# Logarithms of 2048 small matrices: Jacobi sweeps replaced by simultaneous turns of all pairs, as 32x32 products on TensorE

## The chip, the cores and the metric

The kernel runs on one core of one Trainium2 chip, in f32 except where said. The metric is device time in microseconds. Before the change the median of 3 runs is 18,431.96 us (18,423.55 to 18,440.54).

## The reference, cut to what matters

```python
x = x + _L0_conv_ref(_gn(x), gamma, beta)        # x: 16 x 128 x 32 x 32
t = _to_tokens(x)
t = t + _L1_attn_ref(_ln_t(t), Wq, Wk, Wv, Wo, bo)
t = t + _L1_ffn_ref(_ln_t(t), ...)

def _L0_conv_ref(X, gamma, beta):
    Xf = X.reshape(B * K, s, s)                  # 2048 matrices, 32 x 32
    w, V = jnp.linalg.eigh(Xf)                   # takes the symmetric part
    w = jnp.clip(w, 1e-8)
    L = jnp.einsum('nij,nj,nkj->nik', V, jnp.log(w), V)
    mean_log = jnp.mean(L, axis=0)
    Lc = gamma * (L - mean_log) + beta
    return the same with exp in place of log, of Lc
```

`_gn` is a group normalisation over 4 channels. The attention (top 32 of 1024 keys) and the layer of experts are the same in both kernels.

## The kernel before, in words

The five engines run programs of their own, which wait on semaphores; the order on each engine is the written one. `hold(eng, sem, value)` (line 56) is a wait and an increment of a counter, two instructions. Loops are hardware loops (`Fori`) on each engine. A matmul in f32 stands in the trace as two records, each with a weight load of its own; in bf16 as one.

`normalise` (line 148) loads x as 128 channels x 16 images x 1024 elements, computes the group statistics, adds the transpose, scales, and takes the column norms of every matrix twice (`column_norms`, line 111), to shift the diagonal.

`jacobi` (line 230) works on all 2048 matrices at once, one channel to a partition, in two halves of 8 images: 6 sweeps of 31 turns, each turn rotating 16 disjoint pairs of columns. DVE forms the products of paired columns (line 329), PE sums them over the rows by 32 products with the identity (line 390), POOL and ACT compute the rotation's coefficients on small tiles (lines 435 to 517), DVE applies them (lines 342 and 352) to six images of a half and PE with ACT to two (lines 401 and 428).

`logarithm` (line 530) takes the eigenvalues from the column norms, scales the columns, turns the layout (line 616: four images to the 128 partitions, 32 rows each) and forms each logarithm as a product of 32x32 (`quad_products`, line 636: 16 columns blocks x 4 blocks of rows, 64 products of 32x32 to a bank). At its end DVE sums over all matrices (line 605).

`exponential` (line 646) uses the same `quad_products` in 16 tiles of 128 matrices with 10 steps of 2 halves (64 products each): a polynomial and seven squarings. `back_to_channels` (line 764) turns the layout back. Attention and experts follow.

Of the kernel before, what the change touches and what calls it, by code (L numbers as in the profile page):

```python
# [17 lines left out]
BY_PE = 2  # L18
PAIRS = S // 2
ROUNDS = S - 1  # L20
SWEEPS = 6
# [3 lines left out]
TINY = 1e-30  # L25
TINY_LOG = 1e-18
# [51 lines left out]
def constants(nc, mem):  # L78

    with ExitStack() as ctx:  # L80
# [4 lines left out]
        def _(pool):  # L85
# [3 lines left out]
            nc.gpsimd.memset(mem.tiny[:], TINY).then_inc(filled, 1)  # L89
            nc.gpsimd.memset(mem.eps_gn[:], EPS_GN).then_inc(filled, 1)  # L90
            for tile, value in ((mem.minus_tiny, -TINY), (mem.tiny_log, TINY_LOG), (mem.one, 1.0), (mem.two, 2.0)):
                nc.gpsimd.memset(tile[:], value)
            hold(pool, filled, 5)
# [6 lines left out]
            hold(pool, filled, 7)  # L100
# [3 lines left out]
            for d in range(-3, 4):  # L104
                hold(pool, filled, 8 + d + 3)
                nc.gpsimd.affine_select(out=mem.quad_mean[:], in_=mem.quad_mean[:], compare_op=ALU.not_equal,
                                        fill=1.0 / (B * P), base=S * d, pattern=[[-1, P]],
                                        channel_multiplier=1).then_inc(filled, 1)

def column_norms(nc, mem, sems, base):

    squares_ready, squares_used, norms_summed = sems

    def act_part(act, source_ready, ready_at, norms_ready):
        for c in range(4):
            act.wait_ge(source_ready, ready_at[c // 2])
            if c >= 2:  # L120
                act.wait_ge(norms_summed, base * 4 + c - 1)
            nc.scalar.activation(mem.product[c % 2][:, :].rearrange("p (m n) -> p m n", m=4),
                                 mem.even[:, 4 * c:4 * c + 4, :], ACT.Square).then_inc(squares_ready, 1)
            if c >= 1:
                collect(act, c - 1, norms_ready)
        collect(act, 3, norms_ready)

    def collect(act, c, norms_ready):
        act.wait_ge(norms_summed, base * 4 + c + 1)
        nc.scalar.activation(mem.weights[:, c // 2, 0, 4 * (c % 2):4 * (c % 2) + 4, :],  # L130
                             mem.dots[c % 2][:, 0:4 * S].rearrange("p (m j) -> p m j", m=4),
                             ACT.Copy).then_inc(norms_ready, 1)

    def pe_part(pe, norms_ready, ready_base):
        for c in range(4):
            hold(pe, squares_ready, base * 4 + c + 1)
            if c >= 2:
                hold(pe, norms_ready, ready_base + c - 1)
            sq = mem.product[c % 2][:, :].rearrange("p (mj r) -> p mj r", r=S)
            for r in range(S):  # L140
                last = nc.tensor.matmul(mem.dots[c % 2][:, 0:4 * S], mem.ident[:], sq[:, :, r],
                                        start=(r == 0), stop=(r == S - 1))
            last.then_inc(norms_summed, 1)

    return act_part, pe_part

def normalise(nc, mem, x_dram):

    with ExitStack() as ctx:
# [5 lines left out]
        norm_sems = (sem("prep_squares"), None, sem("prep_norms"))  # L157
        norms_ready = sem("prep_norms_ready")
        sums = ctx.enter_context(nc.sbuf_tensor("sums", [P, 4, B], F32))
        ps = mem.dots[0]  # L160
# [7 lines left out]
        @block.tensor  # L168
        def _(pe):
            hold(pe, step, 1)  # L170
            nc.tensor.matmul(ps[:, 0:B], mem.group[:], sums[:, 0, :], start=True, stop=True).then_inc(pe_done, 1)
            pe.wait_ge(squared, B)
            nc.tensor.matmul(ps[:, B:2 * B], mem.group[:], sums[:, 1, :], start=True, stop=True).then_inc(pe_done, 1)
            column_norms(nc, mem, norm_sems, 0)[1](pe, norms_ready, 0)
            column_norms(nc, mem, norm_sems, 1)[1](pe, norms_ready, 4)

        @block.scalar
        def _(act):
            act.wait_ge(step, 2)
            scratch = mem.work[:].rearrange("p s (m n) -> p (s m) n", n=N)  # L180
            for m in range(B):
                if m >= 12:
                    act.wait_ge(squared, m - 11)
                nc.scalar.activation(scratch[:, m % 12, :], mem.even[:, m, :], ACT.Square,
# [3 lines left out]

            column_norms(nc, mem, norm_sems, 0)[0](act, step, (6, 6), norms_ready)
            act.wait_ge(step, 7)  # L190
            nc.scalar.activation(sums[:, 3, :], sums[:, 2, :], ACT.Sqrt, bias=mem.tiny[:]).then_inc(act_done, 1)

            column_norms(nc, mem, norm_sems, 1)[0](act, step, (9, 9), norms_ready)

        @block.vector
        def _(dve):
# [21 lines left out]
            dve.wait_ge(norms_ready, 4)  # L218
            for h in range(2):
                last = nc.vector.tensor_reduce(sums[:, 2, HB * h:HB * h + HB], mem.weights[:, h, 0], AX.X, ALU.add)  # L220
            last.then_inc(step, 1)
            dve.wait_ge(act_done, 2)
            nc.vector.tensor_scalar(mem.shift[:], sums[:, 3, :], 1.1, 1e-4, ALU.mult, ALU.add).then_inc(step, 1)
            dve.wait_ge(step, 8)
            diag = mem.even[:, :, 0:N:S + 1]
            nc.vector.tensor_tensor(diag, diag, mem.shift[:].rearrange("p (m n) -> p m n", n=1).broadcast_to([P, B, S]),
                                    ALU.add).then_inc(step, 1)

def jacobi(nc, mem):  # L230

    with ExitStack() as ctx:
# [3 lines left out]
        def small(name, *shape):  # L241
            return ctx.enter_context(nc.sbuf_tensor(name, [P, 2] + list(shape), F32))

        twice_dot = small("twice_dot", HB, PAIRS)
        weighed = small("weighed", HB, 2, PAIRS)
        cross = small("cross", HB, PAIRS)
        half_cross = small("half_cross", HB, PAIRS)
        gap = small("gap", HB, PAIRS)
        radicand = small("radicand", HB, PAIRS)
        root = small("root", HB, PAIRS)  # L250
        gap_abs = small("gap_abs", HB, PAIRS)
        gap_sign = small("gap_sign", 2, HB, PAIRS)
        inverse = small("inverse", HB, PAIRS)
        ratio = small("ratio", 2, HB, PAIRS)
        coef = small("coef", HB, 2, PAIRS)
        secant = small("secant", HB, PAIRS)
        cosine = small("cosine", HB, PAIRS)
        moved = small("moved", 2, HB, S)
        scale = small("scale", HB, S)

        prod_ready = [sem(f"prod_ready{h}") for h in range(2)]
        dots_done = [sem(f"dots_done{h}") for h in range(2)]
        dot_read = [sem(f"dot_read{h}") for h in range(2)]
        cross_ready = [sem(f"cross_ready{h}") for h in range(2)]
        gap_ready = [sem(f"gap_ready{h}") for h in range(2)]
        root_ready = [sem(f"root_ready{h}") for h in range(2)]
        sum_ready = [sem(f"sum_ready{h}") for h in range(2)]
        inverse_ready = [sem(f"inverse_ready{h}") for h in range(2)]
        act_step = sem("act_step")
        coef_ready = [sem(f"coef_ready{h}") for h in range(2)]  # L270
        sec_ready = [sem(f"sec_ready{h}") for h in range(2)]
        cos_ready = [sem(f"cos_ready{h}") for h in range(2)]
        moved_ready = [sem(f"moved_ready{h}") for h in range(2)]
        weights_ready = [sem(f"weights_ready{h}") for h in range(2)]
        part_ready = [sem(f"part_ready{h}") for h in range(2)]
        rotated_ready = [sem(f"rotated_ready{h}") for h in range(2)]
        rotated_out = [sem(f"rotated_out{h}") for h in range(2)]
        ones_ready = sem("ones_ready")
        left_over = sem("left_over")
        scale_log = sem("scale_log")  # L280
        scale_ready = sem("scale_ready")
        scaled = sem("scaled")
        norms_ready = sem("norms_ready")
        norm_sems = (sem("squares_ready"), None, sem("norms_summed"))
        dve_step, pool_step = sem("dve_step"), sem("pool_step")
        DVE_STEPS, POOL_STEPS, ACT_STEPS = 8, 18, 6

        def columns(buf, h):
            return buf[:, HB * h:HB * h + HB, :].rearrange("p m (j r) -> p m j r", r=S)

        def paired(buf, h):
            return buf[:, HB * h:HB * h + HB, :].rearrange("p m (s j r) -> p m s j r", s=2, r=S)

        def swapped(t):
            return t[:, :, ::-1]

        def over_sides(t):
            return t.rearrange("p m (s j) -> p m s j", s=1).broadcast_to([P, HB, 2, PAIRS])

        def twice(t):  # L300
            return t.rearrange("p m (s j) -> p s m j", s=1).broadcast_to([P, 2, HB, PAIRS])
# [1382 lines left out]
```

## Time and profile before

| | us |
|---|---|
| median of 3 runs | 18,431.96 |
| span of the profiled execution | 18,450.5 |
| Jacobi turns | 11,292.3 |
| exponential | 1,300.2 |
| PE busy over the span | 13,662.3 |
| DVE busy over the span | 10,991.9 |

The execution that was profiled has its span, from first to last instruction, as its only time; it stands 18.5 us over the median of the runs. Busy times of PE are modelled at their ends and overlap with its weight loads (PEld).

### The profile page before, as it was taken

What the parts mean: (1) busy time and instruction counts of PE and PEld (TensorE: products, weight loads), DVE (VectorE), ACT (ScalarE), POOL (GpSimd) and SP (SyncE); (2) the same over time, 40 slices, a digit from 0 to 9 for tenths busy, and PEclk for the clock granted to TensorE, in tenths of its full rate; (3) what the DMA queues carried; (4) which work ended last, traced back from release to release, by engine and by line L of the source; (5) the groups of instructions that cost most, each with busy time, mean ns of one, the idle gap of its engine ahead of it and who ended that gap; (6) DMA issues with size and microseconds to landing.
All of it is one profiled execution on the core that took longest, in us unless ns stands there. A gap on an engine that the chain in (4) does not pass through costs nothing. (4 is left out here: it accounts for less than half of the span.)

```text
span 18450.5 us, 246828 instructions
## 1 busy us (share of the span) xinstructions
PE 13662.3 (74%) x91050; PEld 8655.1 (47%) x91050; DVE 10991.9 (60%) x12977; ACT 4604.4 (25%) x10433; POOL 7006.3 (38%) x5640
## 2 busy tenths in 40 slices
PE   5777777777777777777777776444688888888888
PEld 5555555555555555555555555444322222222222
DVE  5777677767776777677767776111335445454454
ACT  2222222222222222222222222111233333333333
POOL 3666566656665666566656664000000000000000
PEclk9888888888888888888888888555789989999899
DMA  0000000000000000000000000000000000000000
GB/s 19 0 0 0 0 0 0 0 0 0 0 0 0 0 0 0 0 0 0 0 0 0 0 0 0 4 4 4 22 3 2 2 3 2 3 2 2 3 2 3
DMA packets 10095, 37.45 MB, mean 2 GB/s; under 512 B 1525, under 2 KB 3130, under 8 KB 9274
## 3 DMA queue, kind: packets, MB, share of 16 engines
q1 hardware_dynamic: 9274, 26.02, 0.4%
q8 instruction: 574, 9.40, 0.2%
q14 instruction: 247, 2.02, 0.0%
HBM read 17.63 MB, written 8.39 MB: 1 GB/s over the span
## 5 line engine op out<-in xcount | busy, mean ns | idle before, releaser
L390 PE MATMUL psum<-work,ident 128*128 128x128 f32 x23808 | 5351.9, 400 | 2810.3 <-DVE work L329 2810.3
L390 PEld LDWEIGHTS psum<-work,ident 128*128 128x128 f32 x23808 | 4999.1, 239 | 3314.4 <-issue 3100.0
L1326 DVE MAX8 w_best<-psum 128x8 f32<-128x128 f32 x8192 | 1696.3, 280 | 1012.2 <-PE psum L1221 1010.4
L491 POOL TENSOR_TENSOR gap<-weights 128x128 f32<-128x128 f32 x372 | 1955.6, 5257 | 866.5 <-ACT weights L465 472.8
L1276 PE MATMUL psum<-w_exp,w_v 128*32 128x512 f32 x4096 | 2125.5, 621 | 8.5 <-ACT w_exp L1305 7.0
L342 DVE TENSOR_TENSOR work<-even,coef 128x2048 f32<-128x2048 f32 (+1 forms) x384 | 1824.4, 4787 | 149.6 <-POOL coef L503 126.9
L329 DVE TENSOR_TENSOR work<-even 128x3072 f32<-128x3072 f32 (+1 forms) x384 | 883.8, 2305 | 1568.4 <-ACT even L428 1231.3
L342 DVE TENSOR_TENSOR work<-odd,coef 128x2048 f32<-128x2048 f32 x360 | 1718.1, 4811 | 0.0
L1305 ACT ACTIVATE w_exp<-psum 128x512 f32<-128x512 f32 x2048 | 1211.8, 597 | 1753.3 <-PE psum L1247 1753.3
L329 DVE TENSOR_TENSOR work<-odd 128x3072 f32<-128x3072 f32 x360 | 828.9, 2302 | 1306.0 <-ACT odd L428 1279.5
L401 PE MATMUL psum<-work,ident 128*128 128x512 f32 x2976 | 1524.7, 594 | 0.0
L352 DVE TENSOR_TENSOR odd<-even,work 128x384 f32<-128x384 f32 (+1 forms) x576 | 1446.8, 2562 | 26.5 <-DVE work L342 0.2
L352 DVE TENSOR_TENSOR even<-odd,work 128x5376 f32<-128x5376 f32 x540 | 1353.9, 2558 | 26.5
L493 POOL TENSOR_TENSOR weighed<-weights,twice_dot 128x256 f32<-128x256 f32 x372 | 353.0, 949 | 1993.6 <-ACT twice_dot L440 1993.6
L499 POOL TENSOR_TENSOR root<-root,gap_abs 128x128 f32<-128x128 f32 x372 | 889.0, 2390 | 386.7 <-ACT root L445 386.7
L517 POOL TENSOR_TENSOR moved<-weights,cosine 128x256 f32<-128x256 f32 x372 | 986.9, 2653 | 66.4 <-POOL cosine L516 66.4
L401 PEld LDWEIGHTS psum<-work,ident 128*128 128x128 f32 x2976 | 566.5, 190 | 718.5 <-issue 718.5
L401 PE MATMUL psum<-even,ident 128*128 128x512 f32 x1536 | 796.8, 600 | 76.6 <-DVE work L342 76.6
L1247 PE MATMUL psum<-w_q,w_k 99*128 99x512 bf16 x2048 | 806.1, 400 | 42.7 <-ACT w_q L1316 42.7
L1221 PE MATMUL psum<-w_k,w_q 96*128 96x512 bf16 x2048 | 631.1, 390 | 205.1 <-ACT w_q L1316 116.0
L1247 PEld LDWEIGHTS psum<-w_q,w_k 99*128 99x128 bf16 x2048 | 200.5, 98 | 1197.8 <-issue 1104.7
L641 PE MATMUL psum<-power 32*32 32x32 f32 x28672 | 450.9, 237 | 417.6 <-issue 401.0
(280 smaller groups left out, 13542.3 us busy)
## 6 DMA issues: line engine op xcount, KB each, us to landing
odd<-in_x SPq DMA_DIRECT2D x1, 8192.0 KB, 22.9
even<-in_x SPq DMA_DIRECT2D x1, 8192.0 KB, 24.0
out<-w_t SPq DMA_DIRECT2D x16, 512.0 KB, 4.5
w_hid<-in_fc SPq DMA_DIRECT2D x2, 256.0 KB
w_wo<-in_wo SPq DMA_DIRECT2D x8, 8.0 KB
w_wq<-in_wq SPq DMA_DIRECT2D x1, 64.0 KB
w_wk<-in_wk SPq DMA_DIRECT2D x1, 64.0 KB
w_wv<-in_wv SPq DMA_DIRECT2D x1, 64.0 KB
```

Of the source, the lines that this page charges most:

```text
L329: nc.vector.tensor_tensor(product[:, which], g[:, which, 0], g[:, which, 1], ALU.mult)\
L342: ins = nc.vector.tensor_tensor(part[:, which], partner[:, which], cb[:, which], ALU.mult)
L352: ins = nc.vector.tensor_tensor(to, a, b, ALU.add)
L390: last = nc.tensor.matmul(mem.dots[h][:, 0:P], mem.ident[:], pr[:, :, r], start=(r == 0), stop=(r == S - 1))
L401: last = nc.tensor.matmul(to, mem.ident[:], of[:, m, side].rearrange("p j r -> p (j r)"), start=(n == 0), stop=(n == 1))
L491: nc.gpsimd.tensor_tensor(gap[:, h], norm[:, :, 1], norm[:, :, 0], ALU.subtract).then_inc(gap_ready[h], 1)
L499: nc.gpsimd.tensor_tensor(root[:, h], root[:, h], gap_abs[:, h], ALU.add).then_inc(sum_ready[h], 1)
L517: nc.gpsimd.tensor_tensor(mv[:, 1], w, over_sides(cosine[:, h]), ALU.mult).then_inc(moved_ready[h], 1)
L1247: nc.tensor.matmul(banks[4 + m % 3][:], w.k[0:DEPTH + SHIFT_ROWS, 4 * g + j, P * kt:P * kt + P], w.q[0:DEPTH + SHIFT_ROWS, 4 * g + j, QB * ...
L1276: nc.tensor.matmul(banks[7][slot(j), :], w.v[:, kt, 4 * g + j, :], w.exp[m % 4][:], start=(kt == 0), stop=(kt == KT - 1)).then_inc(s.weigh ...
L1305: nc.scalar.activation(w.exp[m % 4][:], banks[4 + m % 3][:], ACT.Exp).then_inc(s.exp_done, 1)
L1326: last = nc.vector.max(w.best[:, i, o, :], banks[2 * (i % 2) + o // 4][:, P * (o % 4):P * (o % 4) + P])
```

## The change

The Jacobi sweeps, the column norms, the shift and the old logarithm are taken out. The new stage (`eigen`) first turns the layout, so that four matrices stand over each other in the 128 partitions, and works on tiles of 64 matrices (128x512). There are 4 groups of 8 tiles. Each tile gets 14 turns. In a turn, for all pairs of a matrix at once: gap and damping of each pair (two full products and two sets of 64 small ones, one of them in bf16), an angle matrix X by Ln and Exp, an orthogonal matrix J as a polynomial in X (Gram and turn: a full bf16 product and a set of 64 small ones each), then A J, J^T A J twice over for symmetry (a set and two sets), and U J (a set). Matrices in the last turn but one get a correction of U's orthogonality ("mended"). The stages of a turn are spread over slots: while tile t is at its gap, tile t-1 is at its angle, t-2 at its Gram, and so on to t-5; each engine's program goes through the slots in the written order. The turns run in two loops of 5 and 6 iterations with four bodies written out beside them, each body 8 slots. At the end of a group the logarithm is formed from U and the scaled U. The scaling in `normalise` writes `odd` in place of `even`. `exponential` and all behind it are unchanged. The diff, cut to its core:

```diff
-def column_norms(nc, mem, sems, base):
...
-            column_norms(nc, mem, norm_sems, 0)[1](pe, norms_ready, 0)
-            column_norms(nc, mem, norm_sems, 1)[1](pe, norms_ready, 4)
...
-            nc.vector.tensor_tensor(mem.even[:], mem.odd[:],
+            nc.vector.tensor_tensor(mem.odd[:], mem.odd[:],
...
-def jacobi(nc, mem):
...
-def logarithm(nc, mem):
...
+TILE = 16
+W = TILE * S
+TG = 8
+GROUPS_E = B * P // (4 * TILE * TG)
+FIRST_DAMP, LATER_DAMP = 0.25, 0.125
+FIRST_TURNS, LATER_TURNS = 6, 8
+TURNS = FIRST_TURNS + LATER_TURNS
...
+GAP, DAMP, GRAM, TURN, PROD, NEXT, VECT, MEND = range(8)
...
+def quads(nc, bank, left, right, start=True):
+    for k in range(TILE):
+        cols = slice(S * k, S * k + S)
+        for q in range(4):
+            rows = slice(S * q, S * q + S)
+            last = nc.tensor.matmul(bank[rows, cols], left[rows, cols], right[rows, cols], start=start, stop=True,
+                                    skip_group_check=not start)
+    return last
...
+AT_ANGLE, AT_GRAM, AT_TURN, AT_PROD, AT_NEXT = 1, 2, 3, 4, 5
+def slots(base, before, now):
+    def at(j, delay):
+        kind = now if j >= delay else before
+        return None if kind is None else (base + (j - delay), (j - delay) % TG, kind)
+    for j in range(TG):
+        yield j, lambda delay, j=j: at(j, delay)
...
+        def turns(eng, g, body):
+            base = g * PER
+            body(eng, g, base, None, PLAIN, 0)
+            with eng.Fori(1, FIRST_TURNS) as i:
+                body(eng, g, base + i * TG, PLAIN, PLAIN, 0)
+            with eng.Fori(FIRST_TURNS, MEND_AT) as i:
+                body(eng, g, base + i * TG, PLAIN, PLAIN, 1)
+            body(eng, g, base + MEND_AT * TG, PLAIN, MENDED, 1)
+            body(eng, g, base + (MEND_AT + 1) * TG, MENDED, PLAIN, 1)
+            body(eng, g, base + TURNS * TG, PLAIN, None, 1)
...
+            def turn(pe, g, base, before, now, which):
+                for j, at in slots(base, before, now):
+                    if at(AT_PROD) is not None:
+                        m, t, kind = at(AT_PROD)
+                        if kind == MENDED:
+                            hold(pe, mend_out, g * TG + t + 1)
+                        else:
+                            hold(pe, turned, m + 1)
+                        if not (before is None and j == AT_PROD):
+                            hold(pe, prod_out, m)
+                        quads(nc, banks[PROD], e.a[t], e.j[t % 4]).then_inc(prod_done, 1)
+                    if at(AT_NEXT) is not None:
+                        m, t, kind = at(AT_NEXT)
+                        if at(AT_PROD) is None:
+                            hold(pe, prod_out, m + 1)
+                            hold(pe, vect_out, m)
+                        turned_by = e.j[t % 4]
+                        for k in range(TILE):
+                            cols = slice(S * k, S * k + S)
+                            for left, right, first in ((turned_by, e.prod[t % 2], True), (e.prod[t % 2], turned_by, False)):
+                                for q in range(4):
+                                    rows = slice(S * q, S * q + S)
+                                    last = nc.tensor.matmul(banks[NEXT][rows, cols], left[rows, cols], right[rows, cols],
+                                                            start=first, stop=not first)
+                        last.then_inc(next_done, 1)
+                        quads(nc, banks[VECT], turned_by, e.u[t]).then_inc(vect_done, 1)
+                    if at(AT_TURN) is not None:
+                        m, t, kind = at(AT_TURN)
+                        hold(pe, mixed, m + 1)
+                        nc.tensor.matmul(banks[TURN], e.turn_eye[:], over_matrices(e.eye_bf[:]), start=True, stop=True)
+                        quads(nc, banks[TURN], e.zs[t % 2], e.mix[t % 2], start=False).then_inc(turn_done, 1)
+                        if kind == MENDED:
+                            hold(pe, turned, m + 1)
+                            hold(pe, mend_ready, g * TG + min(t + AT_TURN, TG))
+                            quads(nc, banks[MEND], e.mend[t % 4], e.j[t % 4]).then_inc(mend_done, 1)
+                    if at(AT_GRAM) is not None:
+                        m, t, kind = at(AT_GRAM)
+                        hold(pe, angle, m + 1)
+                        nc.tensor.matmul(banks[GRAM], e.gram_eye[:], over_matrices(e.eye_bf[:]), start=True, stop=True)
+                        quads(nc, banks[GRAM], e.x[t % 4], e.x[t % 4], start=False).then_inc(gram_done, 1)
+                    if at(0) is not None:
+                        m, t, kind = at(0)
+                        hold(pe, diag_ready, m + 1)
+                        if not (before is None and j == 0):
+                            hold(pe, damped, m)
+                        nc.tensor.matmul(banks[GAP], e.block_ones[:], e.diag[t % 2], start=True, stop=True)
+                        quads_by(nc, banks[GAP], e.diag[t % 2], e.minus_ones, start=False).then_inc(gap_done, 1)
+                        hold(pe, off_ready, m + 1)
+                        nc.tensor.matmul(banks[DAMP], e.damp[which][:], e.off[t % 2], start=True, stop=True)
+                        quads_by(nc, banks[DAMP], e.off[t % 2], e.damp_rows[which], start=False).then_inc(damp_done, 1)
+                        if kind == MENDED:
+                            hold(pe, flipped, g * TG + t + 1)
+                            if t >= AT_TURN:
+                                hold(pe, mend_out, g * TG + t - AT_TURN + 1)
+                            quads(nc, banks[MEND], e.flip[t % 2], e.flip[t % 2]).then_inc(length_done, 1)
...
+            def turn(act, g, base, before, now, which):
...
+                        act.wait_ge(damped, m + 1)
+                        nc.scalar.activation(e.damped[t % 2], e.damped[t % 2], ACT.Ln, bias=e.floor[:]).then_inc(log_taken, 1)
...
+                        act.wait_ge(next_done, m + 1)
+                        nc.scalar.activation(e.square[:, t], banks[NEXT], ACT.Square, scale=0.5)
+                        nc.scalar.activation(e.a[t], banks[NEXT], ACT.Copy, scale=0.5).then_inc(next_out, 1)
...
+                        act.wait_ge(log_taken, m + 1)
+                        nc.scalar.activation(e.damped[t % 2], e.damped[t % 2], ACT.Exp, scale=-1.0).then_inc(inverse, 1)
...
+                        act.wait_ge(prod_done, m + 1)
+                        nc.scalar.activation(e.prod[t % 2], banks[PROD], ACT.Copy).then_inc(prod_out, 1)
...
+                        act.wait_ge(gram_done, m + 1)
+                        nc.scalar.activation(e.zs[t % 2], banks[GRAM], ACT.Copy, scale=THIRD).then_inc(gram_out, 1)
...
+                        act.wait_ge(gap_done, m + 1)
+                        nc.scalar.activation(e.gap_sq[t % 2], banks[GAP], ACT.Square).then_inc(gap_squared, 1)
...
+            def turn(dve, g, base, before, now, which):
...
+                        dve.wait_ge(vect_done, m + 1)
+                        nc.vector.tensor_copy(e.u[t], banks[VECT]).then_inc(vect_out, 1)
...
+                        dve.wait_ge(turn_done, m + 1)
+                        nc.vector.scalar_tensor_tensor(e.j[t % 4], e.x[t % 4], ANGLE_PART, banks[TURN], ALU.mult, ALU.add)\
+                            .then_inc(turned, 1)
...
+                        dve.wait_ge(gram_out, m + 1)
+                        nc.vector.scalar_tensor_tensor(e.mix[t % 2], banks[GRAM], FOURTH / THIRD, e.x[t % 4], ALU.mult,
+                                                       ALU.add).then_inc(mixed, 1)
...
+                        dve.wait_ge(inverse, m + 1)
+                        dve.wait_ge(weighed, m + 1)
+                        nc.vector.tensor_tensor(e.x[t % 4], e.weighed[t % 2], e.damped[t % 2], ALU.mult).then_inc(angle, 1)
...
+                        dve.wait_ge(gap_squared, m + 1)
+                        nc.vector.tensor_tensor(e.weighed[t % 2], e.a[t], banks[GAP], ALU.mult).then_inc(weighed, 1)
+                        dve.wait_ge(damp_done, m + 1)
+                        nc.vector.tensor_tensor(e.damped[t % 2], e.gap_sq[t % 2], banks[DAMP], ALU.add).then_inc(damped, 1)
...
+                    nc.gpsimd.tensor_tensor(as_matrices(e.diag[t % 2]), as_matrices(e.a[t]), over_matrices(e.eye[:]), ALU.mult)\
+                        .then_inc(diag_ready, 1)
+                    nc.gpsimd.tensor_tensor(as_matrices(e.off[t % 2]), as_matrices(e.square[:, t]), over_matrices(e.not_eye[:]),
+                                            ALU.mult).then_inc(off_ready, 1)
```

Left out are the constants, the way into and out of a group, and DVE's part of the mending.

## Rows read from the trace of the kernel before

**Rows 1.** The page's header.

```profile
span 18450.5 us, 246828 instructions
```

**Rows 2.** Windows: start:end, length, busy time (instructions) by engine, clock, DMA.

```profile
236.70:11529.00 11292.30, 8264.15 (x31307) 6465.32 (x31308) 8188.77 (x2671) 2444.23 (x6777) 6982.09 (x5582) 0.85 0.00 0
11529.00:11736.50 207.50, 94.48 (x4345) 89.72 (x4345) 61.39 (x26) 28.46 (x48) 1.89 (x10) 0.60 0.01 3
11736.50:13036.70 1300.20, 644.92 (x40960) 597.42 (x40960) 135.00 (x127) 172.06 (x288) 0.00 (x0) 0.50 0.02 4
```

**Rows 3.** The page's groups of instructions: count, busy, mean ns, idle before.

```profile
L390 PE MATMUL psum<-work,ident 128*128 128x128 f32 x23808 | 5351.9, 400 | 2810.3 <-DVE work L329 2810.3
```

**Rows 4.** DMA queues, Jacobi turns, then exponential: packets, MB, share.

```profile
q8 instruction: 6, 0.10, 0.0%
...
q8 instruction: 349, 5.72, 1.8%
```

**Rows 5.** Timeline of PE in the exponential: start, length, what, idle before.

```profile
11759.48 1.99 PE L641 MATMUL psum<-power 32*32 32x32 f32 x127 [0.67 <-issue]
...
11799.14 1.93 PE L641 MATMUL psum<-power 32*32 32x32 f32 x127 [1.50 <-issue]
...
11814.79 0.44 PE L641 MATMUL psum<-a 32*32 32x32 f32 x16 [3.65 <-issue]
...
12166.03 1.99 PE L641 MATMUL psum<-power 32*32 32x32 f32 x127 [0.68 <-issue]
...
12176.77 1.95 PE L641 MATMUL psum<-power 32*32 32x32 f32 x127 [1.53 <-issue]
12180.81 1.97 PE L641 MATMUL psum<-power 32*32 32x32 f32 x127 [2.08 <-issue]
...
12206.47 1.92 PE L641 MATMUL psum<-power 32*32 32x32 f32 x127 [1.50 <-issue]
```

**Rows 6.** Timeline of the logarithm, and the window of its first burst (clock 1.00).

```profile
11586.29 1.27 PE L641 MATMUL psum<-work 32*32 32x32 f32 x128 [1.99 <-issue]
11589.75 1.93 PE L641 MATMUL psum<-work 32*32 32x32 f32 x128 [2.19 <-issue]
11593.20 2.00 PE L641 MATMUL psum<-work 32*32 32x32 f32 x127 [1.52 <-issue]
...
11586.20:11587.60 1.40, 1.27 (x128) 1.16 (x128) 0.08 (x1) 0.00 (x0) 0.00 (x0) 1.00 0.04 12
```

**Rows 7.** Line 641: durations in ns (least, median, most), first and last start.

```profile
L641 PE MATMUL psum<-power x28672: 225/236/258, 11758.4 to 13035.4; 32*32 32x32 f32 x200
```

**Rows 8.** Groups of ACT, DVE and POOL: count, busy, mean ns, idle before.

```profile
L742 ACT ACTIVATE power<-psum 128x512 f32<-128x512 f32 x192 | 114.7, 598 | 723.8 <-PE psum L641 723.8
L724 DVE TENSOR_TENSOR power<-psum,low 128x512 f32<-128x512 f32 x32 | 22.1, 691 | 84.8 <-PE psum L641 84.8
L501 POOL TENSOR_TENSOR ratio<-inverse,gap_sign 128x256 f32<-128x256 f32 x372 | 268.9, 723 | 352.1 <-ACT inverse L449 352.1
L491 POOL TENSOR_TENSOR gap<-weights 128x128 f32<-128x128 f32 x372 | 1955.6, 5257 | 866.5 <-ACT weights L465 472.8 <-ACT weights L130 393.3 <-POOL weights L521 0.4
L787 ACT ACTIVATE work<-odd 128x4096 f32 x4 | 28.5, 7136 | 44.3 <-PE psum L799 43.9 <-PEq L653 0.4
```

**Rows 9.** Full products: timeline in a turn, and a group of bf16 ones.

```profile
11016.33 1.02 PE L401 MATMUL psum<-work,ident 128*128 128x512 f32 x2
11017.19 1.02 PE L401 MATMUL psum<-odd,ident 128*128 128x512 f32 x2
...
L1221 PE MATMUL psum<-w_k,w_q 96*128 96x512 bf16 x2048 | 631.1, 390 | 205.1 <-ACT w_q L1316 116.0 <-DVE w_best L1326 75.2 <-DVE w_k L1206 13.9
```

**Rows 10.** Timeline of normalising and of the logarithm.

```profile
95.37 17.22 DVE L215 TENSOR_TENSOR even<-odd,sums 128x16384 f32<-128x16384 f32 x1
...
11571.95 10.09 PE L616 MATMUL psum<-ident,work 128*128 128x128 f32 x64 [7.97 <-DVE work L599]
...
11702.45 27.46 DVE L605 TENSOR_REDUCE factor<-odd 128x32 f32<-128x16384 f32 x1
```

More of the change, by code:

```diff
@@ L251, in jacobi @@
[L251 to L262, printed above, removed]
@@ L321, in _ @@
+        @block.tensor
+        def _(pe):
+            pe.wait_ge(filled, 8)
+            nc.tensor.matmul(e.banks[0][:, 0:P], e.block_ones[:], triangle[:], start=True, stop=True).then_inc(summed, 1)
         @block.vector
         def _(dve):
-            def products(h, buf, put_at=None):
-                g = paired(buf, h)
-                product = mem.product[h][:, :].rearrange("p (m j r) -> p m j r", m=HB, r=S)
-                for which in (mine, others):
-                    if which is others and put_at is not None:
-                        dve.wait_ge(rotated_out[h], put_at)
-                    nc.vector.tensor_tensor(product[:, which], g[:, which, 0], g[:, which, 1], ALU.mult)\
-                        .then_inc(prod_ready[h], 1)
@@ new lines, in _ @@
+            nc.vector.tensor_reduce(e.ramp[:, 0:1], triangle[:], AX.X, ALU.add).then_inc(ramped, 1)
+            dve.wait_ge(ramped, 1)
+            scale = 2.0 / sum(n * n for n in range(1, S + 1))
+            nc.vector.tensor_scalar(e.ramp[:, 1:2], e.ramp[:, 0:1], scale, -scale * (S + 1), ALU.mult, ALU.add)\
+                .then_inc(ramped, 1)
+            dve.wait_ge(ramped, 2)
+            dve.wait_ge(summed, 1)
+            nc.vector.scalar_tensor_tensor(e.mirror[:], e.banks[0][:, 0:P], e.ramp[:, 1:2], mem.ident[:], ALU.mult, ALU.add)\
+                .then_inc(ramped, 1)
@@ L545, in logarithm @@
[L545 to L550 removed]
+        staged, cut, cut_act, cut_dve = (sem(n) for n in ("e_staged", "e_cut", "e_cut_act", "e_cut_dve"))
@@ L628, in _ @@
-            nc.tensor.matmul(banks[0][:, 0:S], mem.quad_mean[:], factor[:, 0, :], start=True, stop=True)\
-                .then_inc(averaged, 1)
+                    last.then_inc(cut, 1)
+                hold(pe, cut_act, g * 4 + 4)
+                hold(pe, cut_dve, g * 4 + 4)
+                for t in range(TG + 1):
+                    if t < TG:
+                        quads_by(nc, banks[PROD], e.a[t], e.mirror_rows).then_inc(begun_prod, 1)
+                    if t >= 1:
+                        if t >= 2:
+                            hold(pe, begun, g * TG + t - 1)
+                        nc.tensor.matmul(banks[NEXT], e.mirror[:], e.prod[(t - 1) % 2], start=True, stop=True)\
+                            .then_inc(begun_next, 1)
+                    if t < TG:
+                        hold(pe, begun_out, g * TG + t + 1)
@@ new lines, in end @@
+            def end(g):
+                for t in range(TG):
+                    hold(pe, raised, g * TG + t + 1)
+                    if t >= 2:
+                        hold(pe, (formed_act, formed_dve)[t % 2], g * (TG // 2) + (t - 2) // 2 + 1)
+                    quads(nc, banks[t % 2], e.u[t], e.x[t % 4] if t < 4 else e.j[t % 4]).then_inc(formed, 1)
+                hold(pe, formed_act, (g + 1) * (TG // 2))
+                hold(pe, formed_dve, (g + 1) * (TG // 2))
+            with pe.Fori(0, GROUPS_E) as g:
+                begin(g)
+                turns(pe, g, turn)
+                end(g)
@@ L631, in _, with turn @@
         @block.gpsimd
         def _(pool):
+            def turn(pool, g, base, before, now, which):
+                for j, at in slots(base, before, now):
+                    if at(0) is None:
+                        continue
+                    m, t, kind = at(0)
+                    if before is None:
+                        hold(pool, begun, g * TG + t + 1)
+                    else:
+                        hold(pool, next_out, m - TG + 1)
+                    if not (before is None and t < 2):
+                        hold(pool, damp_done, m - 1)
+                    nc.gpsimd.tensor_tensor(as_matrices(e.diag[t % 2]), as_matrices(e.a[t]), over_matrices(e.eye[:]), ALU.mult)\
+                        .then_inc(diag_ready, 1)
+                    nc.gpsimd.tensor_tensor(as_matrices(e.off[t % 2]), as_matrices(e.square[:, t]), over_matrices(e.not_eye[:]),
+                                            ALU.mult).then_inc(off_ready, 1)
@@ L633, in _, with cut_to @@
+            with pool.Fori(0, GROUPS_E) as g:
+                turns(pool, g, turn)
             hold(pool, averaged, 1)
+def cut_to(e, b):
+    t = e.arena_a.rearrange("p (k r) -> p k r", r=S)
+    return t[:, :, 4 * b:4 * b + 4]
 def quad_products(nc, bank, left, right, first):
```

613 lines of the change are left out of this document (243 added, 370 removed).

## The prediction

> **What bounds the kernel now.** I read the windows by stage first [rows 2]. The span of 18,450.5 us [rows 1] falls into 236.7 us of normalising, 11,292.3 us of Jacobi turns, 207.5 us of logarithm, 1,300.2 us of exponential, and 5,413.8 us for the way back and the attention layer. The change replaces the second and third parts and shortens the first; the rest, 18,450.5 - 11,736.5 = 6,714 us, has the same code in both kernels. 11,292.3 us over 186 turns is 60.7 us a turn. The column of that row shows no engine full: PE 8,264 us, DVE 8,189, POOL 6,982. The dot products on PE wait 2,810 us for DVE, and run 5,352 us [rows 3]: the turn is a ring through all engines. So the question is not which engine was slow, but what the new stage costs per product.
>
> The second view is that of the DMA queues. In the 11,292 us of Jacobi turns the queue that carries PE's instructions (q8) moved 6 packets; in 1,294 us of the exponential it moved 349, of 16 KB each (5.72 MB / 349) [rows 4]. The Jacobi loop on PE holds two turns: 2 x 160 matmul records, and as many weight loads, 640 instructions and some waits, and it is not fetched again as it turns. The exponential's loop holds 10 steps x 2 halves x 64 products; an f32 product is two records (40,960 records in that window [rows 2], which is 16 x 20 x 64 x 2), each with its weight load: 5,120 instructions, and it is fetched anew every time. 81,920 instructions of 64 bytes are 320 packets of 256 instructions; 349 were moved.
>
> The third view, the timeline of the exponential, shows what this means [rows 5]. PE runs 127 records (half of 256, less a wait) in 1.96 to 2.00 us and then stands still, with "issue" as the reason, until the next 127. From 11,759.48 to 11,799.14 there are 11 such bursts: 3.605 us each; from 12,166.03 to 12,206.47 there are 11: 3.676 us. The longest spacing is 4.04 us, the shortest in the logarithm 3.45 [rows 5, 6]. The mean of the 22 is 3.64 us. It is not the array: in the logarithm the same 128 records took 1.27 us with the clock granted at 1.00 (2.4 GHz) and 1.93 us later, the time that the exponential's bursts take at 0.50 (1.2 GHz) [rows 2, 5]; the next burst came 3.46 us and 3.45 us after the start of the one before [rows 6]. It is not the data either: ACT's copy of a half takes 0.6 us [rows 8] and falls into the other half's burst or the stillness before it. So small products in a loop that is fetched anew cost what their instructions cost to bring in: 3.64 us per 256 instructions.
>
> **The new stage, counted in instructions.** One tile (64 matrices, 128x512) in one turn issues on PE 7 x 64 small f32 products (gap, Gram, turn, product, two for next, vectors): 896 records. One set of 64 is in bf16: 64 records, one each. One full 128x512 f32 product: 2 records. Three full bf16 ones: 3. Together 965 records, and, since in the rows weight loads equal matmuls in number [rows 2], 965 loads: 1,930 instructions. Seven holds of two instructions each give 1,944. There are 4 groups x 14 turns x 8 tiles = 448 of these: 870,912. Per group there are besides: the way in (64 records of 128x128, 8 x 64 products, 8 full ones, holds) 2,256 instructions; the mending in one turn (2 x 8 x 64 products) 4,144; the way out (8 x 64 products) 2,080; times 4, 33,920. Sum 904,832, or 3,535 packets.
>
> A jump back costs more. In the exponential 349 packets were moved where the instructions and holds (82,560) fill 322.5: 26.5 over 16 turns of the loop, 1.66 each; the rows show it as a packet of which only 16 records are used [rows 5]. The new stage has 4 + 5 jumps back in a group and one of the outer loop, 40: 66 packets. Total 3,601 packets x 3.64 us = 13,108 us. The ends are the shortest and the longest spacing: 12,423 and 14,548 us.
>
> **What lies beside it.** For one tile and turn PE needs 7.6 packets, 27.7 us. ACT has 7 passes of 128x512 at 0.60 us, 4.2 us; DVE 6 at 0.69, 4.1 us; POOL two products of 128x512, for which no row stands: 128x256 took 0.72 us, so 1.5 us each from below; from above 5.3 us each, as the 128x128 one of line 491, which runs beside DVE, took in the mean. At most 10.5 us [rows 8]. Each is off the path, because every result is used a slot (27 us) later than it is made. PE's own array time is 896 x 15.4 ns = 13.8 us at 1.2 GHz, 1.0 for the bf16 set, 2 x 0.86 for the f32 full one (0.43 us per record at the higher clock [rows 9], doubled; I take the lower clock, as the exponential has) and at most 3 x 0.4 for the others [rows 9]: 17.7 us, hidden under 27.7. The cover ends only if the fetch were faster than 17.7 / 7.6 = 2.3 us a packet.
>
> **What is not hidden.** At each group's start ACT lays out 128x4096, 7.1 us [rows 8]; the transposes run at the pace of line 616, 10 us for 64 records [rows 10], some 8 over their fetch; the levels, logarithm and scaling on DVE and ACT before the way out some 7, filling and draining the pipeline and the way in's chain some 15. I take 37 us a group, between 0 and 100: 150 us. Before it, normalising now ends with the scaling that in the rows ends at 95.37 + 17.22 = 112.6 us [rows 10]; the column norms, some 124 us, are gone; ten for the constants give 123. After it the sum over all matrices stays at 27.5 us [rows 10], with its products 30.
>
> **Sum.** 123 + 13,108 + 150 + 30 + 6,714 = 20,125 us of span. The median of the runs shown is 18.5 us under the profiled span (18,431.96 against 18,450.5), so 20,110 us: 9.1% slower. By the ends of the spacing it is 19,422 and 21,547, and 250 more if the groups' edges cost 100 each. The whole exponential gives 1,300.2 / 349 = 3.73 us a packet with its short chains, which would make 20,420. I keep 3.64, since the new stage has no such chain.
>
> **A rule against it.** The bursts of 127 with 1.5 to 2.1 us between them [rows 5] say that fetching is in the open. The Trainium skill (Runtime: NRT & Kernel Launch, Instruction fetch mechanics) says that the sequencer fetches the next block of 256 instructions while it runs the present one, and that crossing a block is "mostly hidden". By that rule the time would be that of the first rival; by the row it is the forecast. This case's trace agrees on the 256 instructions and disagrees on the hiding.
>
> **The rivals.** (1) The array sets the pace, because in a long straight body the fetch runs ahead: 17.7 us a tile and turn at the lower clock, x 448 = 7,930 us, with the groups' ends (132 packets of 2 us) 260, and the other terms 7,017: 15,200 us, faster by 17%; at the higher clock, 1.27 / 1.93 of it, about 12,500. For it: half of the stretch is "issue", which names no cause. Against it: the bodies of the exponential and the logarithm are straight too, 20 and 8 bursts long, and show no burst that comes early. It decides from 3.17 us a packet on: (18,450.5 - 7,017) / 3,601. No spacing between whole bursts in the rows is below 3.45. Chance 0.11, with all between it and the forecast. (2) Products that add to what a product just before has written (the second half of "next", line for line behind the first) wait for its end, 237 ns by the mean of a record [rows 7]: 16 such waits are 3.8 us a tile and turn. Hidden under the fetch this is nothing; if waiting PE stops the fetch, it is 448 x 3.8 = 1,700 us: 21,800 us. For it: the order within a column block. Against it: the fetch went on at 3.46 us while the array was busy for 1.27 or 1.93. Chance 0.04. (3) The passes on ACT, DVE and POOL hold PE up: that needs more than 27.7 us of a chain in a slot, where I count 10.5 at most. Chance 0.02, some 21,000 to 23,000. (4) That the shorter normalising and the lost ring just balance it, within 0.2% (about what runs of this kernel tell from no change): 0.01.
>
> **How the numbers follow.** Forecast 0.82, 20,110 us. The range 19,400 to 21,400 takes in the shortest spacing and nearly the longest; it leaves out rival 1 and the rest. Faster 0.11; same 0.01; slower 0.88, from the forecast and the rivals 2 and 3.
>
> **What would show it.** Some 3,600 packets of q8 during the new stage, 3.4 to 4.0 us apart; bursts of about 127 records with "issue" between them; PE's idle time under "issue" and hardly any under ACT, DVE or POOL; 27 to 29 us from one tile to the next; the granted clock near 0.50; the exponential unchanged at 1,300 us. It is wrong if the bursts of 127 join, if fewer packets than a tenth under that number are moved, or if PE waits for a semaphore in each slot.

## The result, and the profile after

The changed kernel takes 20,251.6 us (median of 4 runs, 20,224.4 to 20,260.5) against 18,436.3 us of the kernel before (median of 4): a ratio of 1.0982 (1.0967 to 1.0998), slower by 9.8%. The profiled execution has a span of 20,220.8 us.

Windows of the changed kernel (columns as in [rows 2]): the eigenvalue stage, the exponential.

```profile
118.80:13463.90 13345.10, 8319.49 (x449026) 6544.15 (x449026) 1957.43 (x2925) 1920.10 (x3305) 1068.82 (x906) 0.56 0.02 4
13463.90:14833.80 1369.90, 646.92 (x40960) 596.30 (x40960) 136.47 (x128) 171.97 (x288) 0.00 (x0) 0.50 0.02 4
```

13,345 us stand where Jacobi turns and logarithm took 11,500 [rows 2]. DVE has fallen from 8,189 us in the turns to 1,957, POOL from 6,982 to 1,069; PE's busy time is the same (8,319 us against 8,359), with over twelve times the records (449,026 against 35,652). DMA queue q8 over the eigenvalue stage, the answer to [rows 4]:

```profile
q8 instruction: 3579, 58.64, 1.8%
```

3,579 packets where the Jacobi turns moved 6: one every 3.73 us. A packet itself is under way for about 1.07 us of these (1.8% of 16 engines' 13,345 us, over 3,579); what fills the rest, no view shows. Who PE waited for (us in all, times, longest):

```profile
PE psum L304 <- issue: 2867.7, 1949, 5.1
PE psum L423 <- issue: 1567.6, 896, 2.7
PE psum L656 <- issue: 672.8, 334, 5.0
PE psum L315 <- issue: 360.1, 264, 2.3
PE psum L1236 <- ACT w_q L1331: 116.0, 48, 2.5
```

The first wait for another engine stands fifth, and belongs to the attention. Within the eigenvalue stage PE waits 4,823 us under "issue" and 171 us for other engines. The longest of these (line 607 is the scaling before the way out of a group):

```profile
PE psum L304 <- DVE even L607: 52.1, 4, 13.0
PE psum L304 <- DVE even L559: 37.3, 36, 1.1
```

PE's timeline in one slot (line 304 holds the small products, 439 and 446 full ones), answering to [rows 5]:

```profile
5020.24 1.65 PE L304 MATMUL psum<-e_mix,e_zs 32*32 32x32 f32 x105
5022.95 0.54 PE L304 MATMUL psum<-e_mix,e_zs 32*32 32x32 f32 x23 [1.06 <-issue]
5023.42 0.61 PE L439 MATMUL psum<-e_eye_bf,e_gram_eye 128*128 128x512 bf16 x1
5023.96 1.60 PE L304 MATMUL psum<-even 32*32 32x32 f32 x103
5026.65 0.57 PE L304 MATMUL psum<-even 32*32 32x32 f32 x25 [1.09 <-issue]
5027.16 2.08 PE L446 MATMUL psum<-even,e_block_ones 128*128 128x512 f32 x2
```

A set of 128 records is cut after 105, the next after 103, each time with "issue" as the reason; the rest of each starts 3.70 us after the other (5,022.95 to 5,026.65), which is the pace of the packets.

### The profile page after: what moved, and what is told of

The parts are those of the page before. It is cut to its first block and busy times, and to the rows that moved or that the text cites. A ratio compares the mean times of both kernels' runs of the same rounds, so it can differ in the third digit from the quotient of the medians.

```text
span 20220.8 us, 1057271 instructions
## 1 busy us (share of the span) xinstructions
PE 13487.9 (67%) x503916; PEld 8539.7 (42%) x503916; DVE 4706.3 (23%) x13219; ACT 4020.5 (20%) x6897; POOL 1092.1 (5%) x957
## 5 line engine op out<-in xcount | busy, mean ns | idle before, releaser
L304 PE MATMUL psum<-even 32*32 32x32 f32 x176128 | 2892.8, 231 | 2384.1 <-issue 2308.0
L304 PEld LDWEIGHTS psum<-even 32*32 32x32 f32 x176128 | 2568.5, 144 | 2741.1 <-issue 2704.1
L423 PE MATMUL psum<-even,e_prod 32*32 32x32 f32 x57344 | 1756.1, 236 | 808.4 <-issue 808.4
L423 PE MATMUL psum<-e_prod,even 32*32 32x32 f32 x57344 | 1750.8, 236 | 762.7 <-issue 759.2
L423 PEld LDWEIGHTS psum<-e_prod,even 32*32 32x32 f32 x57344 | 1603.5, 150 | 899.4 <-issue 899.4
L423 PEld LDWEIGHTS psum<-even,e_prod 32*32 32x32 f32 x57344 | 1603.3, 150 | 798.1 <-issue 798.1
L304 PE MATMUL psum<-e_mix,e_zs 32*32 32x32 f32 x57344 | 987.3, 237 | 469.3 <-issue 469.3
L304 PEld LDWEIGHTS psum<-e_mix,e_zs 32*32 32x32 f32 x57344 | 868.9, 150 | 724.3 <-issue 724.3
L446 PE MATMUL psum<-even,e_block_ones 128*128 128x512 f32 x896 | 913.8, 1123 | 11.5 <-DVE even L581 4.8
L315 PE MATMUL psum<-e_minus_ones,even 32*32 32x32 f32 x57344 | 809.0, 225 | 8.9 <-issue 7.9
```

What stands on the lines that cost most here:

```text
L304: last = nc.tensor.matmul(bank[rows, cols], left[rows, cols], right[rows, cols], start=start, stop=True, skip_group_check=not start)
L315: last = nc.tensor.matmul(bank[rows, cols], left[rows, cols], right[rows, :], start=start, stop=True, skip_group_check=not start)
L423: last = nc.tensor.matmul(banks[NEXT][rows, cols], left[rows, cols], right[rows, cols], start=first, stop=not first)
L446: nc.tensor.matmul(banks[GAP], e.block_ones[:], e.diag[t % 2], start=True, stop=True)
```

## The experiments

Theory A: PE lives on what its instructions cost to bring in. Rival B: the array's time. The stages were cut as above in every trace. Each variant ran once, except the two timed at the end. The first four share a chip, the next four another. The unchanged eigenvalue stage took 13,345 us in the trace above, 13,459 on the first of these chips and 13,526 on the second, so small differences are read on one chip only.

**More array, hardly more instructions.**

```diff
+                        for _ in range(3):   # gap; 4 for damping, Gram and turn
                             nc.tensor.matmul(banks[GAP], e.block_ones[:], e.diag[t % 2], start=True, stop=True)
```

> The changed kernel with its four full products repeated in every tile and turn (gap 3 times, damping, Gram and turn 4 times each); the results are the same, the first ones are overwritten. Per tile and turn that is 13 records more on PE and 26 instructions, 1.3% of 1,944, but 4 x 0.85 + 9 x 0.43 = 7.3 us more of array time at 1.2 GHz (3.6 us at 2.4). Theory A (PE lives on what its instructions cost to bring in, 3.73 us per 256): 448 x 26 / 256 = 46 packets more, 170 us, so 20,420 us; the array time falls into stillness that is there anyway, though the full products now stand in one piece and some of it may show. Rival B (the array's own time sets the pace): 448 x 7.3 = 3,270 us more, 23,500 us; at the higher clock 1,600 more, 21,850.

Measured: 20,631.7 us. Window of its stage:

```profile
118.80:13896.50 13777.70, 9116.37 (x454850) 6459.69 (x454850) 1978.24 (x2925) 1920.24 (x3305) 1069.60 (x906) 0.71 0.02 4
```

The stage is 318 us longer than the same stage of the kernel with the small loop below, which ran on the same chip (13,459 us); 52 more packets (46 were reckoned) at 3.76 us are 196 of them. Some 120 us are left for array work that made PE busy 778 us longer than there. The granted clock rose from 0.56 to 0.71, so the added work was cheaper than the 7.3 us a tile and turn reckoned at 1.2 GHz. B's smallest figure, 1,600, is missed by far. A's 20,420 us is missed by 212, of which the chip may be 114 (13,459 against 13,345).

**Fewer instructions.** Two sets against constant rows became row sums on DVE:

```diff
-                        quads_by(nc, banks[GAP], e.diag[t % 2], e.minus_ones, start=False).then_inc(gap_done, 1)
-                        quads_by(nc, banks[DAMP], e.off[t % 2], e.damp_rows[which], start=False).then_inc(damp_done, 1)
+                        nc.vector.tensor_reduce(own, as_matrices(e.diag[t % 2]), AX.X, ALU.add)
+                        nc.vector.tensor_reduce(offs, as_matrices(e.off[t % 2]), AX.X, ALU.add)
+                        # gap = bank - own; damped = offs * damp + bank + gap squared
```

> The changed kernel without the two sets of 64 small products against constant rows (one f32, one bf16): what they give is a row sum, which DVE now takes (two reductions and two more passes of 128x512 per tile and turn, some 2.7 us on DVE, which is busy 4.4 of 29). PE issues 384 instructions fewer per tile and turn: 672 packets in all. Theory A: 672 x 3.73 = 2,500 us less, 17,740 us, and q8 moves some 2,910 packets in the stage. Rival B: less by what these products are busy, 809 + 329 = 1,140 us: 19,110 us. Rival C (a chain through ACT and DVE sets the slot): no change or slower.

Measured: 18,002.0 us. Window and q8 of the stage:

```profile
118.80:11188.90 11070.10, 6966.01 (x363010) 5339.44 (x363010) 3010.19 (x4717) 1933.71 (x3305) 1068.57 (x906) 0.58 0.02 4
```

```profile
q8 instruction: 2907, 47.63, 1.8%
```

672 packets fewer, as counted, and 2,389 us less than 13,459; the products had been busy 1,140. The time is 262 us over A's figure and 1,108 under B's. This is already 2.4% under the kernel before on the same chip (18,446 us, one run of each).

**The mirrored half left out.**

```diff
-                            for left, right, first in ((turned_by, e.prod[t % 2], True), (e.prod[t % 2], turned_by, False)):
+                            for left, right in ((turned_by, e.prod[t % 2]),):
```

> The changed kernel with the next matrix taken from the first half of its products alone (J^T times A J), without the second half that adds the mirrored product to it; the scaling by one half goes. 64 small f32 products fewer: 256 instructions per tile and turn, 448 packets. Theory A: 448 x 3.73 = 1,670 us less, 18,580 us. Rival B: less by what these are busy, some 1,750 us, 18,500: this run does not tell A and B apart. It is for the rival that the second half waits for the first in PSUM (16 waits of 0.24 us in a tile and turn, 1,700 us on top): then it is 3,400 us less, 16,850.

Measured: 18,708.1 us; 3,131 packets, 11,818 us. Rival 2 of the prediction, the second half waiting in PSUM, is out: 1,641 us less than 13,459 is what 448 packets cost (3.66 us each), where that rival wanted 3,400. Between A and B this run does not decide.

**The exponential from a small loop.**

```diff
+    with pe.Fori(0, 7):
+        block(0)
+        block(1)
+    block(14)
+    return block(15)
```

> The changed kernel with the exponential's sets of 64 products run from a small loop: column blocks 0 and 1 seven times over, then 14 and 15. As many products, 20 x (32 + 32 + a few) = 1,400 instructions in the loop over tiles instead of 5,160. Blocks 2 to 13 are left out, so the result of the exponential is not the reference's. The eigenvalue stage is as in the changed kernel. Theory A: the queue q8 moves next to nothing in the exponential, and its 1,370 us fall to what array and chain need: 16 x 20 x (1.3 to 2.0 us) = 420 to 640 us, with the short waits for ACT and DVE 500 to 750 us; in all 19,400 to 19,600 us. Rival B: as many products, so 1,370 us and 20,250 in all. Rival D (a jump back costs PE some us each time whatever it jumps to): 16 x 20 x 6 jumps at over 1 us would make the exponential longer than 3,000 us.

Measured: 20,142.8 us; the exponential 1,180.7 us. My theory as I had put it failed here. The queue fell silent, but of 1,370 us only 190 went, where 620 to 870 were expected. q8 in the exponential, and PE's timeline there:

```profile
q8 instruction: 5, 0.08, 0.0%
```

```profile
13603.77 18.62 PE L666 MATMUL psum<-power 32*32 32x32 f32 x656 [1.07 <-ACTq L778]
```

656 records in 18.62 us are 41 rounds of 16 in 0.45 us; at 15.4 ns a record the products are 0.25. So 0.2 us go into each round of the small loop. There are 2,240 rounds (16 x 20 x 7), some 450 us, and without them the exponential would stand at 730, inside what was expected. But that is worked out after the fact: the run could not tell "fetching" from "something as slow", and the next one was made with few jumps.

**The squarings in a loop.** Squarings 3 to 8 as three rounds of two (48 rounds in all):

```diff
+                with pe.Fori(0, 3) as i:
+                    for n in (3, 4):
+                        square(n, t * (2 * STEPS) + i * 4 + 2 * (n - 1), power[(n - 1) % 2], power[(n - 1) % 2])
```

> The changed kernel with the exponential's squarings 3 to 8 as a loop of three times two squarings (1,040 instructions, the same bodies used again), instead of six written out; the same products and results, banks in turns of two. The small loop of the run before this one moved 5 packets instead of 350 and still took 1,181 us, with 0.45 us for every 8 products, where 16 records take 0.24: a jump back to code that is there costs some 0.2 us, and there were 2,240 of them. Here there are 48. Theory A (fetching sets the pace): per tile 3,100 instructions in place of 5,160, 12 to 14 packets at 3.9 us = 47 to 55 us in place of 86, so the exponential takes 750 to 900 us in place of 1,370, and q8 moves 200 to 230 packets in it; in all 19,700 to 19,850 us. Rival B (the array or the chain ACT to PE sets it): 1,370 us again, 20,250.

Measured: 20,021.9 us; the exponential 987 us, 206 packets. PE's timeline in one tile, and the windows of a fetched and of an unfetched stretch:

```profile
13868.09 1.92 PE L656 MATMUL psum<-power 32*32 32x32 f32 x127 [1.80 <-issue]
13871.81 7.09 PE L656 MATMUL psum<-power 32*32 32x32 f32 x547 [1.79 <-issue]
13879.29 5.02 PE L656 MATMUL psum<-power 32*32 32x32 f32 x512 [0.39 <-issue]
...
13868.10:13870.10 2.00, 1.92 (x127) 1.79 (x127) 0.00 (x0) 0.60 (x1) 0.00 (x0) 0.50 0.03 8
13879.30:13884.30 5.00, 4.99 (x512) 4.74 (x512) 0.00 (x0) 2.03 (x4) 0.00 (x0) 1.00 0.00 0
```

This is the cleanest view of the case: the same squarings start a burst of 127 records every 3.7 us as long as they are being fetched (1.9 us of work at a granted clock of 0.50, then stillness), and run 512 in 5.0 us once they are there, with the clock granted at 1.00. Per 127 records that is 1.2 us against 3.7. The clock explains at most 0.7 of the difference, 1.9 against 1.2. The time fell by 383 us, less than the 470 at least that I expected: the two rounds without fetching take some 12 us a tile (13,871.81 to 13,884.31), 200 us in all, which the expectation had left out. The other 790 us are 3.8 for each of the 206 packets.

**A hint for the jump back.**

```diff
+    return nc.Fori(start, end, engines=..., hint_back_edge=eng.engine == mybir.EngineType.PE)
```

> The changed kernel with a prefetch hint for the jump back in PE's loops over turns, groups and the exponential's tiles (one more instruction at the top of each body). Nothing else changes. If each of the 40 jumps back of the eigenvalue stage costs 1.7 packets at 3.75 us, 250 us stand there, and 16 x 6 = 100 us in the exponential. Theory A with a hint that brings the target in ahead: up to 200 + 80 us less, 19,970. If the fetch is one packet after the other, a hint only changes the order: 0 to 50 us less, 20,200 to 20,250. More packets than 3,579 would say that it fetches what it does not use.

Measured: 20,453.3 us; 3,563 packets in the stage and 335 in the exponential, for 13,577 and 1,364 us. Fewer packets (16 and 15), and no time won: on the same chip the stage without the hint took 13,526 us. What a jump costs is not settled by it.

**Fused sets.** U and A J share the stationary J; `pair` is two banks with the blocks of both side by side:

```diff
+                                last = nc.tensor.matmul(e.pair[rows, 2 * S * k:2 * S * k + 2 * S], turned_by[rows, cols],
+                                                        e.arena[rows, first:second + 1:second - first, cols],
+                                                        start=True, stop=True)
```

> The kernel with row sums on DVE, and besides J^T [U | A J] as one set of 64 products with 64 moving columns instead of two sets with 32 (both have J as the stationary side): the same sums, 256 instructions fewer, and their array time only in part. 1,304 instructions per tile and turn, 5.1 packets. Theory A: 448 x 640 / 256 = 1,120 packets fewer than 3,579, 2,459 x 3.78 = 9,300 us for the stage, and 6,760 + 119 for the rest: 16,170 us. The array needs some 16 us of the 19.3 a tile and turn, so the cover is thin: up to 16,700. Rival B (by busy time; the fused set is 64 columns wide): against the run with row sums alone, 18,002, at most the 1.9 us of weight loads and half records: 17,300 to 18,000.

Measured: 16,418.3 us; 2,459 packets as counted, 9,480 us; B's smallest figure was 17,300. This run does not compute the reference's result: most likely the mirrored half was not added to the first, but took its place, which changes no count (see the last section).

**All of it together.**

> All that takes instructions off PE together: row sums on DVE, one set for J^T [U | A J], no mirrored second half of the next matrix (left out as in the run with half of it), squarings in a loop. 1,048 instructions per tile and turn in place of 1,944. Theory A: 448 x 896 / 256 = 1,568 packets fewer, 2,011 x 3.78 = 7,600 us, and the exponential 800 in place of 1,370: 119 + 7,600 + 800 + 5,390 = 13,900 us as long as the array stays under 15.5 us a tile and turn; I count 13 to 14 us for it, and more where waits for ACT and DVE come out (the slot is now only as long as two passes of each): up to 15,000. Rival B: the busy time of the array, which falls by a third: 16,500 or more.

Measured: 14,361.5 us. Stage and q8:

```profile
118.80:7929.80 7811.00, 5024.84 (x247878) 3806.24 (x248322) 3010.36 (x4717) 1934.31 (x3305) 1070.11 (x906) 0.73 0.02 4
```

```profile
q8 instruction: 2011, 32.95, 1.8%
```

Packets as counted; 3.88 us each instead of 3.78. The exponential took 1,010 us where 800 were reckoned. B's 16,500 is missed by 2,100.

**Two versions, timed.**

> Everything that the changed kernel computes, in fewer instructions: row sums on DVE, one set for J^T [U | A J] with the mirrored half added right behind each column block, squarings in a loop. 1,304 instructions per tile and turn, as in the run with fused sets, whose stage took 9,480 us for 2,459 packets; the exponential 987 to 1,010 us as with the squarings in a loop. Theory A: 119 + 9,480 + 1,000 + 5,390 = 15,990 us. A second half that waits for the first in PSUM would show here as more, since only some 3 us of a tile and turn are uncovered: up to 16,400.

Measured: 16,039.0 us, ratio to the kernel before 0.8691 (0.8677 to 0.8706). It computes all that the changed kernel does, with the mirrored half right behind each column block. Its stage took 9,496 us for 2,459 packets, 15 us more than with that half in a set of its own, so no wait in PSUM shows here either:

```profile
118.80:9614.30 9495.50, 6185.17 (x305666) 4695.11 (x305666) 3011.55 (x4718) 1932.69 (x3305) 1068.59 (x906) 0.68 0.02 4
```

> The kernel of the run with the fewest instructions once more, timed in three rounds. 14,360 us, as in its one look, 22% under the kernel before; it leaves out the mirrored second half of the next matrix.

Measured: 14,376.6 us, ratio 0.7791 (0.7778 to 0.7804).

Over five counts of packets the stage took (3,579 from the run with the small loop, 2,459 from the fused one, 2,011 from the run with all of it together; the first, second and third column are from one chip, the last two from another):

| packets | 3,579 | 3,131 | 2,907 | 2,459 | 2,011 |
|---|---|---|---|---|---|
| us | 13,459 | 11,818 | 11,070 | 9,480 | 7,811 |
| PE busy, us | 8,338 | 7,467 | 6,966 | 6,092 | 5,025 |

From first to last that is 5,648 us over 1,568 packets, 3.60 us for each that went. This slope is not the price of a packet, and what it leaves over at no packets, 570 us, is not a fixed cost. The price can be counted directly. In the changed kernel these are the packets of q8 inside the four groups, from 180 to 3,390 us, 3,500 to 6,700, 6,840 to 10,040 and 10,160 to 13,380:

```profile
q8 instruction: 873, 14.30, 1.8%
q8 instruction: 867, 14.20, 1.8%
q8 instruction: 871, 14.27, 1.8%
q8 instruction: 872, 14.29, 1.8%
```

That is 12,830 us over 3,483 packets, 3.68 us each. At this price all 3,579 take 13,184 us, and some 160 us of the stage are left for the groups' edges and the final sum. Counted in the same way, a packet took 3.72 us in the run with the small loop and 3.74 with row sums, on one chip; on the other 3.74 with the squarings in a loop and 3.78 in the run with all together. The price is a little higher in the kernels with fewer packets, and so the slope lies under it. That the array has more to do beside each packet there (PE is busy 2.3 us a packet in the first column, 2.5 in the last) would fit, as would the run with more array; it is not shown by itself.

## Why the prediction was right

**The count.** 3,601 packets were foretold, 3,579 moved: right to 0.6%. In every variant that takes instructions out the difference came out exact (448, 672, 1,120, 1,568), which the run that adds some missed (52 for 46). If the straight code was counted right, the 40 jumps back cost 44 packets and not 66.

**The price.** 3.64 us a packet, read from 22 bursts, against 3.68 counted inside the groups: 0.04 too low, which is less than the same stage differs by from chip to chip (3.68, 3.72, 3.74). The prediction weighed 3.73, the mean of the whole exponential, and set it aside for its short chains; over the whole stage, edges and all, the price came out at just that. The shape was right too: bursts cut at the packets' pace, "issue" as the reason, 27 to 30 us a slot (DVE's copies of U start at 4,989.40, 5,019.82 and 5,047.01 us), the clock granted at 0.56 in the mean of its two levels.

**What lies beside it.** The array hid under the fetch, as [rows 6] let expect: 778 us more of it cost about 120. It does not hide wholly: with the added products a packet inside the groups took 3.75 us, against 3.72 without them on the same chip.

**What is not hidden.** I had 180 us for the edges and the final sum, and some 160 are left for them; PE's waits for other engines, 171 us, agree. The stage came out at 13,345 us against 13,288: 22 packets too many took 80 us off, the price added some 160, the edges took 20. That this stage is right to 0.4% owes something to errors of opposite sign, but each term by itself was right to about a tenth.

**The rest.** I had the exponential unchanged at 1,300 us; it took 1,370, with 350 packets against 349, and 1,352 to 1,402 in the other kernels whose exponential is unchanged. Same code, same count, 5% apart. The 70 us stand in PE's waits under "issue", 672.8 us against 605.0, so the packets came more slowly. That where a loop begins within a packet has a part in it would fit, but was not tried; the cause is open. The parts behind it were 27 us shorter. Together: span 20,221 against 20,125 foretold, and the median lies 31 us over the span, where before it lay 18.5 under.

**The rivals.** Rival 1, the fetch running ahead in a long body, gave 15,200 us; the packets came 3.68 us apart, while the array was busy 2.3 us for each (8,319 us over 3,579). Only in a loop that stays is fetching out of the way, because there is none. The Trainium skill (Runtime: NRT & Kernel Launch, Instruction fetch mechanics) calls the crossing of a block mostly hidden; the traces here disagree wherever code is fetched: a packet took 3.7 us, and its 256 instructions of small products 1.2 to 2.0. Rivals 2 and 3 are refuted by the half set and by PE's list of waits.

## What to carry to other kernels

Before small products are put on TensorE, count instructions, not flops: two for each record, two records for each f32 product, and 3.7 us per 256 of them in a loop too long to stay; the array needed half of that or less. A body of 1,040 instructions stayed and one of 5,160 did not; where between them it ends, no run shows. What lowers the count is what pays: constant sides taken to an idle engine, two products with one stationary side fused, a body short enough to be used again with few jumps. The change's idea was good; with a third of its instructions gone it is 13% faster than the kernel before, not 10% slower.

## What the runs showed that I had not expected

The Trainium skill (PSUM — Partial Sum Buffer, The four PSUM rules) says that a starting product clears the marks of the whole bank in its 32 partitions, and that an adding one then overwrites where the mark is cleared; the two results agree with it.
